# Perceiver block with a 64-expert MoE on one core: down_proj's tail rows loaded as one 128-partition transfer, TensorE filler matmuls ahead of the MoE, and MoE memsets moved late

## What is computed

```python
x = x + cross_attention(layernorm(x), ctx, mask)        # x 256 x 512, ctx 4096 x 512
x = x + self_attention(layernorm(x), w_qkv, w_out)      # 16 heads of 32
# MoE, E = 64 experts, K = 8 of them for each token, H = 512, I = 192
# (in here x is the layernormed x that is passed in)
router_logits = x @ gate_w
routing_weights, selected = jax.lax.top_k(router_logits, K)
routing_weights = jax.nn.softmax(routing_weights, axis=-1)
gate = ragged_dot(hidden_sorted, gate_proj_w, group_sizes)   # 512 -> 192
up   = ragged_dot(hidden_sorted, up_proj_w, group_sizes)     # 512 -> 192
down = ragged_dot(silu(gate) * up, down_proj_w, group_sizes) # 192 -> 512
x = x + ffn(layernorm(x), ...)                          # outputs weighted and summed per token
```

## Time and profile before

| what | value |
|---|---|
| median of 3 runs | 365.71 us (363.33 to 366.94) |
| the profiled execution, its own time | 365.86 us |
| its span, first to last instruction | 364.1 us |
| mean granted TensorE clock | 0.947 |
| PE busy | 320.6 us, 88% |
| DVE, ACT, POOL busy | 161.8, 85.0, 49.3 us |
| DMA packets | 40781, 83.41 MB |

### The profile page before, as it was taken

How to read it: one execution, slowest core, us unless ns; L and a number is a source line. 1 busy time by engine, 2 the same in 40 slices (tenths; PEclk the granted TensorE clock), 3 DMA queues, 4 the chain that set the end, 5 groups by cost and what they waited for, 6 DMA issues and landing times.

```text
span 364.1 us, 9459 instructions
## 1 busy us (share of the span) xinstructions
PE 320.6 (88%) x3302; PEld 179.2 (49%) x3302; DVE 161.8 (44%) x462; ACT 85.0 (23%) x166; POOL 49.3 (14%) x99
## 2 busy tenths in 40 slices
PE   0499999898987488999999999999999999997774
PEld 0363544345763464655565556555655565553332
DVE  8752365964775752324333433343334333432203
ACT  1110302226660412212221222122212221221101
POOL 4000002200000312121111111211121112111100
PEclk9999999997899855999999999999999999999869
DMA  2799999700000005908999829999999999999901
GB/s 63 272 407 351 340 338 315 244 1 2 2 2 0 0 2 176 333 11 279 316 344 343 279 79 339 338 298 318 328 320 322 331 335 332 328 338 329 325 26 58
DMA packets 40781, 83.41 MB, mean 229 GB/s; under 512 B 5672, under 2 KB 14000, under 8 KB 40624
## 3 DMA queue, kind: packets, MB, share of 16 engines
q1 hardware_dynamic: 40336, 82.99, 69.0%
q10 hardware_dynamic: 416, 0.04, 0.1%
HBM read 82.49 MB, written 0.52 MB: 228 GB/s over the span
## 4 chain that ended last, share of the span: by engine, by line
PE 63%; SPq 15%; DVE 11%; issue 5%; ACT 3%; DMA 2%; DVEq 0%; ACTq 0%
PE psum L1159 16%; SPq L372 14%; PE psum L1125 9%; PE psum L1184 8%; PE psum L1094 5%; PE psum L940 4%; PE psum L979 4%; PE psum L952 4%; DMA store<-n_L_ffn_down_proj_w_dram 2%; PE psum L1064 2%; PE psum L931 2%; PE psum L1040 1%; ACT store L854 1%; PE psum L1024 1%; PE psum L1168 1%
## 5 line engine op out<-in xcount | busy, mean ns | idle before, releaser
L1159 PE MATMUL psum<-store 128*32 128x384 f32 x896 | 83.8, 517 | 10.3 <-DMA store<-n_L_ffn_down_proj_w_dram 8.0
L1159 PEld LDWEIGHTS psum<-store 128*32 128x32 f32 x896 | 28.4, 114 | 58.6 <-issue 58.6
L1125 PEld LDWEIGHTS psum<-store 128*128 128x128 bf16 x696 | 40.7, 99 | 20.7 <-issue 11.5
L1125 PE MATMUL psum<-store 128*128 128x128 bf16 x696 | 45.7, 222 | 1.1 <-DVE store L742 0.9
L1184 PE MATMUL psum<-store 128*32 128x256 f32 (+1 forms) x896 | 46.6, 387 | 0.0
L534 POOL TENSOR_TENSOR store<-store 128x256 f32<-128x256 bf16 x28 | 17.2, 614 | 157.4 <-PE psum L1168 156.9
L1094 PE MATMUL psum<-y_parts,place_T 128*128 128x512 f32 x120 | 36.2, 424 | 1.7 <-DVE y_parts L784 1.7
L907 ACT ACTIVATE y_parts<-psum,w_slot 128x512 fp32r<-128x512 f32 x28 | 19.3, 688 | 68.4 <-PE psum L1184 68.4
L782 DVE TENSOR_SCALAR place_T<-psum 128x256 fp32r<-128x256 f32 x28 | 11.9, 425 | 51.5 <-PE psum L1184 51.5
L1184 PEld LDWEIGHTS psum<-store 128*32 128x32 f32 (+1 forms) x896 | 16.7, 107 | 26.6 <-issue 11.5
L902 ACT ACTIVATE store<-psum 128x192 f32<-128x192 f32 x28 | 9.3, 331 | 72.4 <-PE psum L1159 72.4
(11 more groups left out here) (214 smaller groups left out, 322.7 us busy)
## 6 DMA issues: line engine op xcount, KB each, us to landing
store<-n_L_ffn_gate_proj_w_dram SPq DMA_DIRECT2D x64, 384.0 KB, 4.7
store<-in_L_ffn_up_proj_w_dram SPq DMA_DIRECT2D x64, 384.0 KB, 5.0
store<-n_L_ffn_down_proj_w_dram SPq DMA_DIRECT2D x64, 256.0 KB, 5.1
store<-n_L_ffn_down_proj_w_dram SPq DMA_DIRECT2D x128, 64.0 KB, 5.1
store<-in_L_attn_w_qkv_dram SPq DMA_DIRECT2D x1, 3072.0 KB, 14.2
store<-in_ctx_dram SPq DMA_DIRECT2D x2, 1024.0 KB, 6.4
store<-in_L_attn_w_out_dram SPq DMA_DIRECT2D x1, 1024.0 KB, 16.6
x_sb<-in_x_dram SPq DMA_DIRECT2D x1, 512.0 KB, 4.4
```

Source lines behind the costliest of these rows:

```text
L1125: last = pe.matmul(bank[3][:, c * P:(c + 1) * P], xparts[:, h, part, c, :], chosen_slots[:, h], start=(k == 0), stop=(k == 3 * TH - 1))
L1159: last = pe.matmul(bank[0][quarter, 0:2 * INTER], xs[:, c, quarter], w[:, :, c, :], start=(c == 0), stop=(c == DC - 1))
```

## The change

Three things are changed.

1. **Tail rows.** The two 64-partition transfers of down_proj's tail rows become one of 128 partitions: partition 2r holds the left half of tail row r and partition 2r + 1 its right half. DVE writes each tail value of hid twice in neighbouring columns, so the transpose has tail row r in partitions 2r and 2r + 1. On the way out of PSUM DVE makes two masked copies of it, with `side` (1 on even partitions and 0 on odd ones, and the reverse) as a factor. Each half of the output columns is then a matmul over all 128 partitions, with the other half's rows multiplied by zero. The 128 main rows are one matmul of 512 columns for each expert in place of two of 256. The output fits in bank 6. hid's main part has its own semaphore, and the masked copies the new `s_htt`. A team's loads are 16 DMAs in place of 20.
2. **Fillers.** `keep_clock(b, times)` runs bf16 matmuls of 512 columns whose result nobody reads: 3 and 13 before the two waits for the normalized halves, 6 behind the first `mix`, and 6 before PE's wait for the round counts.
3. **Memsets.** `radix`, `lane_radix`, `place_T` and `y_parts` are set behind the self attention in place of the start, with two small reductions that make `side`.

PE's count of rounds of a team goes through a register of its own.

```diff
-        hid_tails = hid[:, P:].rearrange("p (h n) -> p h n", h=2)
-        hidT = carve([P, 2, P])
+        hid_twice = hid[:, P:].rearrange("p (r h) -> p r h", h=2)
+        hidT = carve([P, 3, P])
...
-                                     (lane[0:TAIL_I, TAIL_AT:SLOT_W], down_proj[bass.ds(e, 1), MAIN_I:, 0:D // 2].rearrange("e r n -> (e r) n")),
-                                     (lane[TAIL_I:, TAIL_AT:SLOT_W], down_proj[bass.ds(e, 1), MAIN_I:, D // 2:].rearrange("e r n -> (e r) n"))):
+                                     (lane[:, TAIL_AT:SLOT_W], down_proj[bass.ds(e, 1), MAIN_I:].rearrange("e r (h n) -> (e r h) n", h=2))):
...
-            for q in range(TEAMS // 2):
-                ch.step(dve.memset(radix[:, q::TEAMS // 2], float(8 ** q)), wait=False)
-            for j in range(TEAM):
-                ch.step(dve.memset(lane_radix[:, j::TEAM], float(EXP_N ** j)), wait=False)
-            dve.memset(place_T[:, :].bitcast(F32), 0.0).then_inc(s_mt, 1)
-            dve.memset(y_parts[:, :, :].bitcast(F32), 0.0).then_inc(s_yl, 1)
...
+            for q in range(TEAMS // 2):
+                ch.step(dve.memset(radix[:, q::TEAMS // 2], float(8 ** q)), wait=False)
+            for j in range(TEAM):
+                ch.step(dve.memset(lane_radix[:, j::TEAM], float(EXP_N ** j)), wait=False)
+            dve.wait_ge(s_const, 1)
+            for half in range(2):
+                ch.step(dve.tensor_reduce(side[:, half:half + 1], ident[:, half::2], AX.X, ALU.add), wait=False)
+            dve.memset(place_T[:, :].bitcast(F32), 0.0).then_inc(s_mt, 1)
+            dve.memset(y_parts[:, :, :].bitcast(F32), 0.0).then_inc(s_yl, 1)
...
-                    dve.tensor_tensor(hid_tails, silu[:, MAIN_I:].unsqueeze(1).to_broadcast([P, 2, TAIL_I]),
-                                      bank[0][:, INTER + MAIN_I:2 * INTER].unsqueeze(1).to_broadcast([P, 2, TAIL_I]),
+                    dve.tensor_tensor(hid_twice, silu[:, MAIN_I:].unsqueeze(2).to_broadcast([P, TAIL_I, 2]),
+                                      bank[0][:, INTER + MAIN_I:2 * INTER].unsqueeze(2).to_broadcast([P, TAIL_I, 2]),
                                       ALU.mult).then_inc(s_h, 1)
                     dve.wait_ge(s_htp, v + 1)
-                    dve.tensor_copy(hidT, bank[1][:, 0:2 * P].rearrange("p (k s) -> p k s", k=2)).then_inc(s_ht, 1)
+                    dve.tensor_copy(hidT[:, 0], bank[1][:, 0:P]).then_inc(s_ht, 1)
+                    for half in range(2):
+                        last = dve.tensor_scalar(hidT[:, 1 + half], bank[1][:, P:2 * P], side[:, half:half + 1], None, ALU.mult)
+                    last.then_inc(s_htt, 1)
...
+            def keep_clock(b, times):
+                for _ in range(times):
+                    pe.matmul(bank[b], later_b[:, 0, 0:P], later_b.rearrange("p h t -> p (h t)"), start=True, stop=True)
+
             for h in range(TH):
+                keep_clock(3, 13 if h else 3)
                 pe.wait_ge(s_xn, 2 * TH + h + 1)
                 transpose_half(pe, 6 + h, h)
...
             mix(start=True)
+            keep_clock(3, 6)
...
             last.then_inc(s_tnp, 1)
+            keep_clock(2, 6)

             pe.wait_ge(s_cnt, 3)
...
-                    for k in range(2):
-                        for half in range(2):
-                            for e in range(TEAM):
-                                quarter = slice(e * BLK, (e + 1) * BLK)
-                                rows = slice(0, P) if k == 0 else slice(half * TAIL_I, (half + 1) * TAIL_I)
-                                at = TAIL_AT if k else DOWN_AT + half * (D // 2)
-                                last = pe.matmul(y_half[half][quarter, :], hidT[rows, k, quarter],
-                                                 ring[r][rows, e, at:at + D // 2], start=(k == 0), stop=(k == 1))
+                    for k, (cols, at) in enumerate(((slice(0, D), DOWN_AT), (slice(0, D // 2), TAIL_AT), (slice(D // 2, D), TAIL_AT))):
+                        if k == 1:
+                            pe.wait_ge(s_htt, v + 1)
+                        for e in range(TEAM):
+                            quarter = slice(e * BLK, (e + 1) * BLK)
+                            last = pe.matmul(bank[6][quarter, cols], hidT[:, k, quarter],
+                                             ring[r][:, e, at:at + cols.stop - cols.start], start=(k == 0), stop=(k == 2))
```

More of the change, by code:

```diff
@@ L69, in perceiver @@
         warm = sb("warm", [1, 1])
+        side = sb("side", [P, 2])
         slot_no = sb("slot_no", [P, TOK // BLK, BLK])
@@ L286, in perceiver @@
         s_warm = sem("silu_table_in")
+        s_htt = sem("tails_of_hid_turned")
         s_pk0 = sem("first_pick_written")
@@ L316, in perceiver @@
         block = es.enter_context(nc.Block())
-        y_half = (psum[:, 6, D // 2:], psum[:, 7, 0:D // 2])
-        y_whole = psum[:, 6:8, :].rearrange("p b n -> p (b n)")[:, D // 2:D // 2 + D]
         QK_BANKS = (6, 7, 0, 1)
@@ L783, in _ @@
                     dve.wait_ge(s_yh, v + 1)
-                    dve.scalar_tensor_tensor(y_parts[:, 1], y_whole, w_slot[:, :], y_parts[:, 0], ALU.mult, ALU.subtract).then_inc(s_yl, 1)
+                    dve.scalar_tensor_tensor(y_parts[:, 1], bank[6], w_slot[:, :], y_parts[:, 0], ALU.mult, ALU.subtract).then_inc(s_yl, 1)
                     dve.reg_add(step, step, 1)
@@ L906, in _ @@
                     act.wait_ge(s_ws, v + 1)
-                    act.activation(y_parts[:, 0], y_whole, ACT.Copy, scale=w_slot[:, :]).then_inc(s_yh, 1)
+                    act.activation(y_parts[:, 0], bank[6], ACT.Copy, scale=w_slot[:, :]).then_inc(s_yh, 1)
                     act.reg_add(step, step, 1)
@@ L1140, in _ @@
             last.then_inc(s_tnp, 1)
+            keep_clock(2, 6)
             pe.wait_ge(s_cnt, 3)
             packed = [pe.value_load(packs[0:1, w:w + 1], min_val=0, max_val=8 ** (TEAMS // 2) - 1) for w in range(2)]
+            team_count = pe.alloc_register("pe_team_count")
             step = pe.alloc_register("pe_step")
@@ L1148, in team_rounds @@
                 word, at = divmod(q, TEAMS // 2)
-                count = pe.snap(((packed[word] >> (3 * at)) & 7) + 1, min_val=1, max_val=TOK // BLK)
-                pe.wait_ge(s_w[r], 16 * 5 * TEAM * loads)
+                pe.reg_mov(team_count, ((packed[word] >> (3 * at)) & 7) + 1)
+                count = pe.snap(team_count, min_val=1, max_val=TOK // BLK)
+                pe.wait_ge(s_w[r], 16 * 4 * TEAM * loads)
                 with pe.Fori(0, count):
```

## The result

| | before | after |
|---|---|---|
| median, same chip | 366.32 us (363.33 to 367.71, 4 runs) | 352.69 us (352.55 to 355.16, 4 runs) |
| ratio, 95% interval | | 0.968 [0.961, 0.974] |
| profiled execution, its span | 365.86, 364.1 us | 352.68, 351.0 us |
| granted clock | 0.947 | 0.982 |

The forecast was 350.6, in a range from 346 to 360.5. In the changed kernel gate and up are L1173 (L1159 before), the gather L1136 (L1125), the down matmuls L1197 (L1184), `mix` L1104, the fillers L1083, DVE's copy of hid L780 and its masks L782, its pick of the next tokens L759 (L757).

What follows compares the result with a forecast made beforehand. PE's work was taken to bound the MoE to round 26, the DMA-engine-bound weight stream its end. Round 28 ready at 334.6, plus 0.9 wait, 7.2 and 6.3, gives span 349.0; with 1.8 around it 350.8, forecast 350.6, range 346 to 360.5.

Steps and rivals of the forecast that it cites:

- Start, -1.3: DVE's start: with the memsets moved, the mask's reduction starts sooner, gaining 1.3 us, between 0 and 1.5.
- Memsets and fillers at nothing: Ahead of the MoE: late memsets and fillers fit in idle time of DVE and PE, or beside other work, costing nothing.
- Router -2.0, round 1 -2.2: Up to round 1's end: fillers keep the clock up, gaining 2.0 us before round 1 and 2.2 in it.
- The stream: MoE weight loads: without half-partition transfers the rate rises from 331 to 380 GB/s, 12.4 us a team; last landing 334.3.
- The allowance of 0.9 us for waits: Before round 28: PE ready at 334.6 and the last team landing at 334.3 meet, so 0.9 us of waiting is allowed.
- the half-gain rival: Weight stream: it gains by half, to 350 to 360 GB/s, 13.3 us a team, time 355.5; chance 0.14.
- Masks at nothing: DVE in each round: masks ready by 155.35, before PE wants them at 155.8, so they cost nothing.
- The round, +0.04: PE's down matmuls: full-height tails add 0.04 us a round over 27 rounds, +1.1 us; bounds -0.1 and +0.4 a round.
- Last round 7.2 + 6.3: End of the kernel: round 28 takes 7.2 us, and 6.3 more follow the end of its down matmuls.
- the stream gains nothing: Rival, weight stream: its rate comes from HBM or packet sizes, not partitions, so it stays; 361 us; chance 0.15.
- the clock falls in spite of fillers: Rival, ahead of the MoE: 2.2 + 1.5 us lost and up to 2 for fillers in the way, 354 to 357; chance 0.11.
- The full price of the tails: Rival, PE's rounds: full-height tails cost +0.4 us a round, 9.7 us more in all, 359.5; chance 0.11.

Runs made afterwards that it cites:

- The experiment: The changed kernel without its 28 filler matmuls (the four `keep_clock` calls removed): 357.9 us, ratio 0.975.
- the early pick: The changed kernel with DVE writing the next round's pick right after `w_slot`, not at the head of the next round: 349.75 us, ratio 0.956.
- the half-height transfers: The changed kernel with its interleaved tail rows loaded as two transfers of 64 partitions, PE and DVE as changed: 362.71 us, ratio 0.988.
- thin transfers: The changed kernel with the tail loaded as two transfers of 128 partitions and 512 bytes each: 352.98 us, ratio 0.962.
- the old layout in one transfer: The kernel before with fillers and late memsets, its blocked tail layout loaded by one 128-partition DMA, no masks: 437.85 us, ratio 1.192.
- either half of the fillers: Two kernels with DVE's pick written a round earlier: one with only the 3 and 13 fillers, 353.86 us; one with only the two sixes, 353.3 us.
- fillers in the self attention: The kernel with DVE's pick written a round earlier and all fillers, plus six more fillers in the self attention: 346.07 us, ratio 0.942.
- the last kernel: The kernel with the earlier pick and six self-attention fillers, plus nine more before the output projection: 345.89 us, ratio 0.947.

## Why the prediction was right

Its steps, by the profiled execution.

- **Start, -1.3: right as an effect, lucky as a term of this sum.** The reduction starts 1.40 us sooner, and putting the memsets back moves round 1 by 1.42. But against the kernel before, the output projection starts only 1.02 us sooner (110.61 against 111.63). In between no edit was made, and the lead changes all the same: at the first scores of the self attention it is 2.20 us (78.56 against 80.76), for in the cross attention the first transposes and scores got shorter (3.10 and 3.70 us where they took 3.68 and 4.14). Then the half-clock stretch of the self attention lasts 10.2 us (82.1 to 92.4) where it lasted 6.9 (86.3 to 93.2), and takes 1.2 us back. I had priced neither.
- **Memsets and fillers at nothing.** Right: 1.95 us of DVE's idleness and 0.81 of PE's are left beside them. The 6 behind `mix` delay nothing: the matmuls behind them start at 128.20, 0.06 us after DVE has the chosen experts (128.14). Nor do the last 6: from the round counts (134.75) to round 1 are 1.91 us, and 2.01 in the kernel without fillers. What I had left out is PE's own register for the count of rounds: with the old tail and the old way of counting the same stretch takes 1.64 us (134.76 to 136.40), so it costs about 0.25 us, once.
- **Router -2.0, round 1 -2.2.** From the projection to round 1 are 26.05 us where 28.28 were, and round 1 takes 7.30 in place of 9.44: -2.23 and -2.14. Round 2 was forecast at 143.85 and started at 143.96. The experiment puts the fillers at 5.1 rather than 4.2, but against a round 1 that starts at 139.34, 0.8 us later than 139.91 less the 1.4 of the start. Of that 0.8, 0.55 lies ahead of the projection (110.78 there), in the half-clock stretch told of under the start, and 0.25 is the register.
- **The stream.** That half-height transfers slow it was right; the reason I gave for it is not shown. Taken as 380 GB/s, it was 391; the load of team 11 was issued at 269.95 (forecast 268.6) and the last weights were in before 333 (334.3). The allowance of 0.9 us for waits wasn't needed. By the section "Specifications" of the Trainium skill's page "DMA: Bandwidth & Descriptors" I had given the half-gain rival 0.14; the sustained 391 is above that page's 358 for a core.
- **Masks at nothing.** Right: done at 142.2, where L1197 starts, and its first eight records, of 512 columns each, don't need them.
- **The round, +0.04: the term that was mis-sized.** On PE the sum was right: inside a team, from L1197's start to the next gate and up are 143.96 - 142.22 = 1.74 us, against 156.60 - 154.92 = 1.68. But I priced only PE. The mean of the 26 rounds from 143.96 to 336.95 is 7.42 us, forecast 7.334: +2.3 us.

Where the term comes from shows in a comparison of one change of team in each kernel. Before, then after, from the timelines of all engines:

```profile
315.49 1.66 PE L1184 MATMUL psum<-store 128*32 128x256 f32 x32
317.17 2.79 PE L1159 MATMUL psum<-store 128*32 128x384 f32 x32
...
317.26 0.69 ACT L907 ACTIVATE y_parts<-psum,w_slot 128x512 fp32r<-128x512 f32 x1 [2.45 <-PE psum L1184]
...
319.61 0.29 DVE L757 TENSOR_SCALAR store<-store 128x256 bf16<-128x256 f32 x1 [0.87 <-issue]
319.96 1.53 PE L1125 MATMUL psum<-store 128*128 128x128 bf16 x24
```

```profile
320.11 1.93 PE L1197 MATMUL psum<-store 128*32 128x512 f32 x24
321.86 2.76 PE L1173 MATMUL psum<-store 128*32 128x384 f32 x32
322.11 0.69 ACT L912 ACTIVATE y_parts<-psum,w_slot 128x512 fp32r<-128x512 f32 x1 [2.67 <-PE psum L1197]
...
324.47 0.29 DVE L759 TENSOR_SCALAR store<-store 128x256 bf16<-128x256 f32 x1 [0.89 <-issue]
324.82 1.53 PE L1136 MATMUL psum<-store 128*128 128x128 bf16 x24 [0.20 <-DVE store L759]
```

From ACT's start to the pick's are 2.35 and 2.36 us: that chain didn't change. What changed is its start. The down output reaches ACT 1.77 us after the first down matmul before, and 2.00 after: the full-height tails cost 0.23 us where the output is awaited. PE's next matmuls hide it from PE, whose round starts only 1.75 - 1.68 = 0.07 later. Before, the pick ended at 319.90 and the gather started at 319.96, 2.79 us after the round, where inside a team it starts after 2.72: no slack at all. So the 0.23 less the 0.07 comes out almost whole: the gather now starts 2.96 us after the round, 0.17 later. I had looked at what stood behind DVE's masks, and not at who waits for the end of the down matmuls. It is so in every round: the output reaches ACT after 1.77 us in all 28 before and after 1.99 or 2.00 in all 28 now, and at a change of team the gather started 2.80 us after the round on average, and starts 2.96 us after it now. With the old tail, fillers and late memsets the two are 1.77 or 1.78 and 2.81, so the new tail does it. And the early pick, which takes that step off the chain and brings 4.0 us, shows that PE waited for nothing else.

- **Last round 7.2 + 6.3.** From 336.95 to the end of L1197, 344.68, are 7.7 us: the same wait once more, and the longer L1197. Behind it 6.3 as before. Sum: 349.0 - 0.9 + 2.3 + 0.5 = 350.9, and 0.1 by which round 2 was later than forecast makes the span of 351.0.

Of the rivals, that the stream gains nothing (0.15) is the time of the half-height transfers: 361 forecast, 362.7 measured. That the clock falls in spite of fillers, 354 to 357, is within 1 us of the kernel without them. The full price of the tails (359.5) did not come on PE; about a quarter of it (2.3 of 9.7 us) came by way of ACT and DVE. Rounds didn't get shorter, and the masks weren't late.

## What to carry to other kernels

Two transfers of 64 partitions each cost more here than one of 128 with the same bytes (9.7 us for a ninth of the stream's bytes), and they slowed the large transfers around them as well; bring the data into all 128 partitions, even if the compute side then needs masks or wasted rows. When matmuls are reshaped, price their end as well as their start-to-start time: the next matmuls hide a late end from PE, not from the engine that reads the output, and a chain that had no slack becomes the bound. Idle TensorE time ahead of a dense stretch is worth filling with matmuls that nobody reads, gap by gap; look for the next gap after each one. An effect of 1 or 2 us is read from the traces here: stretches that no edit touches move by as much with the clock.

## What the runs showed that I had not expected

- The stream sustained 391 GB/s over slice after slice once all transfers had full height, and 381 with tail packets of 512 bytes.
- Transfers whose slowest dimension is 2, with one ninth of the bytes (128 of an expert's 1,152 KB), bring the whole stream to 220 GB/s, where half-height transfers gave 330 and full-height ones 391.
- The granted clock isn't the same in executions of one kernel. The same output projection behind the same 2.34 us of idle PE took 7.13 us in eight of the profiles, those of the kernel before, the changed kernel and the early pick among them, and 8.7 to 8.8 in five others (thin transfers, the old layout in one transfer, either half of the fillers, fillers in the self attention); in the last kernel the six times split by about 2 us along with the clock. What tips it, these runs don't show.
